# Attention in a hybrid block, written as one run of 64 items with the projections and the output stage beside them

## What is computed

```python
x = x + _L0_attn_a_ref(_layernorm(x), ...)      # a linear recurrence
x = x + _L0_ffn_ref(_layernorm(x), ...)         # top-k gated layer
x = x + _L0_attn_b_ref(_layernorm(x), ...)      # attention, below
x = x + _L0_ffn_ref(_layernorm(x), ...)

q = (x @ Wq.T).reshape(b, t, N_HEADS, HEAD_DIM)            # 8 heads of 64
kv_latent = x @ Wkv_down.T                                 # rank 64
k = (kv_latent @ Wk_up.T).reshape(b, t, N_HEADS, HEAD_DIM)
v = (kv_latent @ Wv_up.T).reshape(b, t, N_HEADS, HEAD_DIM)
scores = jnp.einsum('bqhd,bkhd->bhqk', q, k) * scale
attn = jax.nn.softmax(scores, axis=-1)
out = jnp.einsum('bhqk,bkhd->bqhd', attn, v)
return out.reshape(b, t, N_HEADS * HEAD_DIM) @ Wo.T
```

## Time and profile before

| | |
|---|---|
| median of 3 runs | 1613.02 us (1611.66 to 1614.74) |
| the profiled execution | 1612.51 us, its span 1610.8 us |
| TensorE busy | 1325.7 us, 82% of the span |
| VectorE busy | 1278.9 us, 79% |
| ScalarE busy | 1105.1 us, 69% |
| GpSimd busy | 1044.0 us, 65% |
| mean granted TensorE clock | 0.935 of full speed |

### The profile page before, as it was taken

One profiled execution on the slowest core, in us unless ns is written; L12 is line 12 of the kernel. 1 busy time (PEld: TensorE's weight loads), 2 busy tenths in 40 slices (PEclk: granted clock), 3 DMA queues, 4 the chain that ended last, 5 costly groups with the idle time before them and its releaser, 6 DMA issues.

```text
span 1610.8 us, 37935 instructions
## 1 busy us (share of the span) xinstructions
PE 1325.7 (82%) x10588; PEld 789.8 (49%) x10588; DVE 1278.9 (79%) x2953; ACT 1105.1 (69%) x2389; POOL 1044.0 (65%) x1234
## 2 busy tenths in 40 slices
PE   5888988767666679998799987999879998867675
PEld 2444444434344335656356663566635666444343
DVE  7988887379999669983689936899368994499997
ACT  3433431777777649995499954999549995888885
POOL 3456565258888738883388842888428885078887
PEclk9999999878988799999999999999999999989997
DMA  6000000000000000000000000000000000000000
GB/s 185 27 1 1 0 0 1 1 1 0 0 0 0 1 1 1 0 1 2 1 1 0 0 2 1 1 0 0 2 1 1 0 0 1 1 14 26 13 26 26
DMA packets 16972, 13.54 MB, mean 8 GB/s; under 512 B 5190, under 2 KB 16652, under 8 KB 16908
## 3 DMA queue, kind: packets, MB, share of 16 engines
q1 hardware_dynamic: 16908, 12.67, 2.6%
HBM read 8.47 MB, written 4.19 MB: 8 GB/s over the span
## 4 chain that ended last, share of the span: by engine, by line
issue 29%; PE 25%; DVE 24%; POOL 9%; ACT 7%; DVEq 3%; SPq 1%; DMA 1%; ACTq 1%; POOLq 0%
DVE arena L1319 5%; DVE arena L1219 4%; DVE arena L1214 4%; PE banks L1674 3%; DVE arena L1127 3%; PE banks L1595 3%; POOL arena L653 3%; PE banks L1614 2%; ACT arena L976 2%; POOL arena L648 2%; PE banks L1616 2%; PE banks L1527 2%; DVE arena L1339 2%; ACT arena L983 2%; PE banks L1580 2%
## 5 line engine op out<-in xcount | busy, mean ns | idle before, releaser
L653 POOL TENSOR_TENSOR arena<-arena 128x512 f16<-128x512 f32 x320 | 405.3, 1275 | 85.2 <-ACT arena L976 84.8
L983 ACT ACTIVATE arena<-banks 128x512 f32<-128x512 f32 x512 | 297.9, 595 | 65.9 <-PE banks L1616 56.2
L1319 DVE TENSOR_REDUCE arena<-banks 128x1 f32<-128x1024 f32 x256 | 307.1, 1216 | 19.6 <-PE banks L1595 10.3
L1339 DVE TENSOR_TENSOR arena<-arena 128x512 f16<-128x512 f32 x192 | 202.5, 1056 | 68.6 <-POOL arena L648 62.9
L976 ACT ACTIVATE arena<-arena 128x512 f16<-128x512 f32 x384 | 233.1, 624 | 0.0
L1629 PE MATMUL banks<-arena 128*128 128x65 f16 x2048 | 217.8, 197 | 13.8 <-POOL arena L653 13.7
L1630 PE MATMUL banks<-arena 128*128 128x64 f16 x2048 | 217.8, 193 | 0.0
L1629 PEld LDWEIGHTS banks<-arena 128*128 128x128 f16 x2048 | 192.2, 98 | 51.3 <-POOL arena L653 30.0
L1631 PE MATMUL banks<-arena 128*128 128x65 f16 x2048 | 216.8, 194 | 0.0
L1614 PE MATMUL banks<-arena 128*128 (+1 forms) x512 | 198.5, 388 | 10.8 <-ACT arena L983 10.8
L1219 DVE MATCH_REPLACE8 arena<-arena 128x256 f32<-128x256 f32 x512 | 205.3, 408 | 0.2
(11 more groups left out here) (196 smaller groups left out, 2931.4 us busy)
## 6 DMA issues: line engine op xcount, KB each, us to landing
x<-in_L_attn_a_x SPq DMA_DIRECT2D x8, 512.0 KB, 3.6
out<-x SPq DMA_DIRECT2D x8, 512.0 KB, 2.9
arena<-in_L_attn_a_W_in SPq DMA_DIRECT2D x1, 768.0 KB, 6.2
arena<-in_L_attn_a_W_mid SPq DMA_DIRECT2D x1, 512.0 KB, 6.9
arena<-in_L_attn_a_w_w SPq DMA_DIRECT2D x2, 256.0 KB, 7.1
arena<-in_L_attn_b_Wq SPq DMA_DIRECT2D x1, 512.0 KB
arena<-in_L_attn_b_Wo SPq DMA_DIRECT2D x1, 512.0 KB
fW<-in_L_ffn_weight SPq DMA_DIRECT2D x1, 256.0 KB
```

The lines of the kernel that those rows point to most:

```text
L653: nc.gpsimd.tensor_tensor(pr_lo[c][:, kt, :], pr[:, kt, :], pr_hi[c][:, kt, :], ALU.subtract).then_inc(a_lP, 1)
L983: nc.scalar.activation(pr[:, kt, :], ps[6 + kt % 2][:, :], ACT.Exp, scale=SM_SCALE).then_inc(a_P, 1)
L1319: nc.vector.tensor_reduce(mx[c][:, j:j + 1], psum[:, 2 * pair:2 * pair + 2, :].rearrange("p a b -> p (a b)"), X, ALU.max).then_inc(a_mx, 1)
L1339: nc.vector.tensor_tensor(pr_lo[c][:, kt, :], pr[:, kt, :], pr_hi[c][:, kt, :], ALU.subtract).then_inc(a_lD, 1)
```

## The change

The loop over batches and the loops inside it are written out: one run of 64 items W on every engine, with no loop instruction and with constants in the waits. The three parts of a batch are laid beside the items:
- The output stage of the batch behind: `FINAL_AT` names the item w of a batch (w = W mod 16) beside which row tile j of the batch behind is done: turned at kt = 1 on TensorE, copied at kt = 3 on ScalarE, multiplied at kt = 4, added at kt = 7 on VectorE.
- The queries of the next pair of heads, four items ahead (`QUERY_AT`, w = 0, 4, 8, 12), into a ring of four heads; turning, keys and latent rows of the batch ahead at w = 9, 10, 11, 13. The half c = 0 has its slot at kt = 1 (TensorE) and kt = 3 (ScalarE and VectorE), c = 1 at kt = 4, kt = 6 and kt = 7.
- The normalised rows of the batch ahead at w = 7 and 8 on ScalarE, kt = 6.
- Keys, latent rows and results (`kA`, `kB`, `latR`, `latL`, `o_sb`) have two buffers.
- The side work takes banks 2 and 3. `max_scores` writes into banks 0 and 1 alone, and waits for `largest_of` of the j right before it.

The prologue makes the projections of batch 0 with the first pair of heads only, and the output stage of batch 3 stands alone at the end as before. In batch 0 there is no output stage beside the items, in batch 3 no projection of a batch ahead. The statistics of the layer norm go straight into their place where the row number is a constant. The steps ahead of attention and behind it are as they were.

```diff
+GROUP = 4
+GROUPS = NH // 2
+Q_RING = 4
...
-        o_sb = xcT[:, :].rearrange("p (t d) -> p t d", t=TIME // P)
+        o_sb = [xcT[:, :].rearrange("p (t d) -> p t d", t=TIME // P), carve([TIME // P, NH * HD])]
...
         MX = TPC
-        Q_BANKS = (2, 3, 6, 7)
-
-
-        FIRST_LARGEST = {1: [(0, 0)], 2: [(0, 1)], 3: [(0, 2)], 4: [(0, 3)], 5: [(1, 0)], 6: [(1, 1)],
-                         7: [(1, 2), (1, 3)]}
-        FIRST_ROWS = 5
+        ALL = BATCH * ITEMS
+        FINALS = TIME // P
+
+
+        FINAL_AT = {1: 0, 2: 1, 3: 2, 5: 3, 6: 4, 7: 5, 14: 6, 15: 7}
+        QUERY_AT = {0: 1, 4: 2, 8: 3, 12: 4}
+        TURN_AT = {9: 0, 10: 1}
+        KEYS_AT, LATENT_AT = 11, 13
...
+            for W in range(ALL):
+                B, w = W // ITEMS, W % ITEMS
+                wait_from(pool, a_ops, W - 1)
+                high(W, 0)
+                low(W, 1)
+                low(W, 2)
+                high(W, 4)
+                if w in QUERY_AT and W + GROUP < ALL:
+                    pool.wait_ge(a_hP, high_done(W, 4))
+                    duplicate(B * GROUPS + QUERY_AT[w], 0)
+                low(W, 3)
+                low(W, 5)
+                if w == 6 and B:
+                    final_rstd(B - 1, 0)
+                if w == 1 and B > 1:
+                    final_rstd(B - 2, 1)
+                low(W, 7)
+                if w in QUERY_AT and W + GROUP < ALL:
+                    pool.wait_ge(a_lP, low_done(W, 7))
+                    duplicate(B * GROUPS + QUERY_AT[w], 1)
+            final_rstd(BATCH - 2, 1)
+            for half in range(2):
+                final_rstd(BATCH - 1, half)
...
+            for W in range(ALL):
+                B, w = W // ITEMS, W % ITEMS
+                onward = B + 1 < BATCH
...
+                    exps(W, kt)
                     if kt - 1 in HIGH_ACT:
-                        high(W, c, kt - 1)
...
+                        high(W, kt - 1)
+                    if kt == 3 and W + 1 < ALL:
+                        max_scaled(W + 1)
+                    if kt in (3, 6):
+                        c = kt // 6
+                        if w in FINAL_AT and B and c == 0:
+                            out_turned((B - 1) * FINALS + FINAL_AT[w], 2)
+                        if w in QUERY_AT and W + GROUP < ALL:
+                            query(B * GROUPS + QUERY_AT[w], c)
+                        if w in TURN_AT and onward:
+                            turned(B + 1, TURN_AT[w], c, 2 + c)
+                        if w == KEYS_AT and onward:
+                            keys(B + 1, c, 2 + c)
+                        if w == LATENT_AT and onward:
+                            latent(B + 1, c, 2 + c)
+                        if w in (7, 8) and onward and c:
+                            attn_rows(B + 1, w - 7)
+                    if kt == 5 and W + 1 < ALL:
+                        max_row(W + 1)
+                high(W, KT - 1)
...
+            for W in range(ALL):
+                B, w = W // ITEMS, W % ITEMS
+                onward = B + 1 < BATCH
...
+                    if kt % 2 == 0 and W + 2 < ALL:
+                        largest_of(W + 2, kt // 2)
...
+                        low(W, kt)
+                    if kt in (3, 7):
+                        c = kt // 7
+                        if w in FINAL_AT and B and c:
+                            final((B - 1) * FINALS + FINAL_AT[w], 3)
+                        if w in QUERY_AT and W + GROUP < ALL:
+                            query_low(B * GROUPS + QUERY_AT[w], c)
+                        if w == KEYS_AT and onward:
+                            keys_low(B + 1, c, 2 + c)
+                        if w == LATENT_AT and onward:
+                            latent_low(B + 1, c, 2 + c)
+                if W:
+                    normalise(W - 1)
+            normalise(ALL - 1)
+            for j in range(FINALS):
+                final((BATCH - 1) * FINALS + j, 6 + j % 2)
+
...
+            def out_final(J, bank):
+                B, j = J // FINALS, J % FINALS
+                pe.wait_ge(a_fe, J + 1)
+                if B == BATCH - 1:
+                    pe.wait_ge(a_fx, J - 1)
+                elif j in (0, 3):
+                    pe.wait_ge(a_ql, (((B + 1) * GROUPS + (1 if j == 0 else 2)) * 2 + 1) * 2 + 2)
...
+                for a in range(NH // 2):
+                    last = mm(ps[bank][:, 0:D], oT[J % 2][:, a, :], voB[:, a, :], start=a == 0,
+                              stop=a == NH // 2 - 1)
+                last.then_inc(a_fm, 1)
+
+            def max_scores(W, j):
+
+                B, hh, c, slot = place(W)
+                if j == 0:
+                    pe.wait_ge(a_kl, B * 2 + 2)
+                    pe.wait_ge(a_dup, query_done(W))
+                wait_from(pe, a_mx, W * MX + j)
                 for half in range(2):
-                    last = mm(ps[2 * pair + half][:, :], qA[:, bass.ds(hh, 1), c * CH + j * P:c * CH + j * P + P],
-                              kA[:, half * CH:half * CH + CH], start=True, stop=True)
+                    last = mm(ps[half][:, :], qA[:, slot, c * CH + j * P:c * CH + j * P + P],
+                              kA[B % 2][:, half * CH:half * CH + CH], start=True, stop=True)
                 last.then_inc(a_mps, 1)
...
+            for W in range(ALL):
+                B, w = W // ITEMS, W % ITEMS
+                onward = B + 1 < BATCH
                 for kt in range(KT):
-                    if kt in LARGEST_AT and largest:
-                        j = LARGEST_AT[kt]
-
-                        read = ((-1, 0, 1, 2) if before else (0, 0, 1, 2))[j]
-                        max_scores(W + 2, hh + 1, c, j, j % 2, read)
-                    scores(W, hh, c, kt)
-                    if kt in WEIGHTED_AT and before:
-                        weighted(W - 1, 1 - c, WEIGHTED_AT[kt])
-                    if kt == 5 and rows:
-                        max_row(W + 1, 1 - c)
...
+                    if kt % 2 == 0 and W + 2 < ALL:
+                        max_scores(W + 2, kt // 2)
+                    scores(W, kt)
+                    if kt in (1, 4):
+                        c = kt // 4
+                        if w in FINAL_AT and B:
+                            J = (B - 1) * FINALS + FINAL_AT[w]
+                            if c:
+                                out_final(J, 3)
+                            else:
+                                out_turn(J, 2)
+                        if w in QUERY_AT and W + GROUP < ALL:
+                            query(B * GROUPS + QUERY_AT[w], c)
+                        if w in TURN_AT and onward:
+                            turn(B + 1, TURN_AT[w], c, 2 + c)
+                        if w == KEYS_AT and onward:
+                            keys(B + 1, c, 2 + c)
+                        if w == LATENT_AT and onward:
+                            latent(B + 1, c, 2 + c)
+                    if kt in WEIGHTED_AT and W:
+                        weighted(W - 1, WEIGHTED_AT[kt])
+                    if kt == 5 and W + 1 < ALL:
+                        max_row(W + 1)
```

More of the change, by code:

```diff
@@ L973, in high @@
+            def high(W, kt):
+                c = W % 2
                 if kt == HIGH_ACT[0]:
-                    act.wait_ge(a_ops, W - 1 + CREDIT["a_ops"])
-                act.wait_ge(a_P, W * KT + (kt + 1 + CREDIT["a_P"]))
+                    wait_from(act, a_ops, W - 1)
+                act.wait_ge(a_P, W * KT + kt + 1)
                 nc.scalar.activation(pr_hi[c][:, kt, :], pr[:, kt, :], ACT.Copy).then_inc(a_hA, 1)
-            def step(W, hh, c, before, rows, largest):
+            for c in range(2):
+                attn_rows(0, c)
@@ new lines, in _ @@
+            for k in range(KB2):
+                turned(0, 0, k, k)
+            for k in range(KB2):
+                turned(0, 1, k, 2 + k)
+            for c in range(2):
+                keys(0, c, 4 + c)
+            for c in range(2):
+                query(0, c)
+            for c in range(2):
+                latent(0, c, 6 + c)
+            max_scaled(0)
+            max_row(0)
+            act.wait_ge(f_x, NT + CREDIT["f_x"])
+            for W in range(ALL):
+                B, w = W // ITEMS, W % ITEMS
+                onward = B + 1 < BATCH
@@ L1590, in max_scores, with turn @@
-            def max_scores(W, hh, c, j, pair=0, read=None):
-                pe.wait_ge(a_mx, W * MX + (j if read is None else read) + CREDIT["a_mx"])
+            def turn(B, c, k, bank):
+                n = LN_ATTN + B * 2 + c
+                pe.wait_ge(s_z, n + 1)
+                if B:
+                    if c == 0:
+                        pe.wait_ge(a_ql, query_done(B * ITEMS - 2 + k))
+                    else:
+                        pe.wait_ge(s_zT, n * 2 - 1 + k)
+                for j in range(TPC):
+                    last = nc.tensor.transpose(ps[bank][:, j * P:j * P + P], z_rows[c][:, j, k * P:k * P + P],
+                                               ident[:, :])
+                last.then_inc(s_tps, 1)
```

(47 more changed lines are left out.)

461 lines of the change are left out of this document (217 added, 244 removed).

## The result

The changed kernel takes 1724.8 us (median of 4 runs, 1722.8 to 1730.3) where the kernel before took 1612.3 in the runs beside it (median of 4, 1610.5 to 1614.7): 1.0702 times as long, 95% interval 1.0673 to 1.0731. The profiled execution took 1722.8 us, its span 1721.1.

What follows compares the result with a forecast made beforehand. Bound: nearly full engines, TensorE kept going by being one `max_scores` ahead of VectorE. Forecast: 1612.5 + 108 (loop with side work) - 9 (start) + 19 (contention) + 40 (clock) = 1770 us; range 1640 to 1840 holds 0.8.

Steps and rivals of the forecast that it cites:

- The bound and the direction: In attention's items, one pair of banks makes TensorE wait for VectorE's first maximum, closing a three-engine loop; slower, chance 0.86.
- the signs that the prediction named: TensorE waiting about 1.9 us at L1736, plain items near 10.4, busy under 80% in items, clock under 0.97.
- The plain period: An item without side work takes 10.4 us instead of 8.65: 6.49 of TensorE's stretch plus 3.95 behind the scores.
- The other maxima don't add: Within an item, maxima after the first cost nothing: 1.8 us each, beside about 2 us of TensorE's work.
- The way over ScalarE: Loop's stretch from kt = 7's scores: 0.26 to the exponential, 0.49 to kt = 6's high part, 0.62 for it.
- The side work: Items take 13.7 us beside outputs (1.1 waiting for oT), 15.1 queries, 11.35 turning, 13.85 keys, 12.85 latent rows.
- The sum: Four batches of items: 197, 228.3 for each full one, 212, less 7; 858 against 750, a loss of 108 us.
- The clock: TensorE at half clock for 3.4 us behind long gaps, 27 times: 40 us taken, bounds 0 and 90.
- The contention: GpSimd's and VectorE's low parts collide at kt = 6: 0 to 0.7 us an item, 0.3 taken, 19 us in all.
- The start and the end: Shorter prologue, with two of eight query products, gains 9 us before the first exponential; nothing forecast for the end.
- Side work hides: Rival: in items only TensorE's 1.75 us adds; 742 us, total 1596 to 1655; chance 0.12 for 1618 to 1690.
- Overlap pays: Rival: maxima don't stall TensorE, whose own work bounds items at 8.65 us; about 1535 us; chance 0.08.

Runs made afterwards that it cites:

- the run without side work: Changed kernel without any side work, one pair of banks: 1520.3 us; its counterpart with two pairs took 1395.3 us.
- first reordered versions: Changed kernel with normalise and next item's first maximum ahead of kt = 6's low part, 1619.5 us; plus copy to oT at kt = 2 and later VectorE side work, 1609.4.
- the one with the early copy alone: Changed kernel with ScalarE's copy of the turned result to oT at kt = 2 instead of kt = 3: 1710.7 us.
- the later ones: Changed kernel, VectorE reordered, plus copy to oT at kt = 2 and later side work, 1609.4 us; plus fourth maximum moved, 1600.7; plus normalised rows singly, 1591.1.
- the reordered versions: Changed kernel with VectorE's first maximum ahead of kt = 6's low part, alone or with further edits: 1619.5, 1609.4, 1600.7 and 1591.1 us.
- the version with the fourth maximum moved: Changed kernel, VectorE reordered, copy to oT at kt = 2, later side work, and fourth maximum ahead of kt = 4's low part: 1600.7 us.

## Why the prediction was right, and where it was not

*The bound and the direction.* Right. One `max_scores` ahead of VectorE was what kept TensorE going: with one pair alone the kernel before loses 102 us, and the run without side work 117 us in its items. Of the signs that the prediction named, one failed and one held barely: TensorE is busy 82 to 83% in the items and not under 80%, and its clock is 0.95 to 0.97 there.

*The plain period.* 10.4 forecast, 10.34 measured; the stretch behind the scores is 3.82 us instead of 3.95. "The other maxima don't add" was wrong. The chain leads over GpSimd and through the fourth maximum into the last low part, and the first `max_scores` waits 0.73 us for that maximum. The way over ScalarE, which the prediction took, is about as long: on ScalarE's timeline the high parts of kt = 6 and 7 start at 638.30 and take 1.14 us together, so the first ends near 638.9, and the low part starts at 638.96 (0.3 us are between the two in the item before). So the number comes out, with some luck: the loop that was forecast is there, but in plain items it is not the one that ended last. In the first reordered versions the fourth maximum is what is left, and costs 0.9 us an item. Whether another order on GpSimd would shorten that way wasn't run.

*The side work.* An item beside an output takes 13.31 us (13.7 forecast), with TensorE waiting 0.8 us at L1724 in 9 of the 24, 1.1 and 1.2 in two others and next to nothing in the rest (1.1 forecast for each). Turning takes 11.33 at w = 10 (11.35), keys 12.84 (13.85). Items with queries take 13.4 to 14.7 and not 15.1 (15.6 to 16.0 at w = 8 and, behind the statistics, at w = 0 of batches 2 and 3), but the stall of their second half falls into the next item, which takes 13.6 to 13.8 where a plain one takes 10.34: the two together 27.0 to 27.7 in batch 0, 25.5 forecast.

*The sum.* The batches took 201.8, 223.5, 228.4 and 204.2 us where 197, 228.3, 228.3 and 205 (212 less the last two items' 7) were forecast: 857.9 against 858. (To the end of the last high part, as the prediction counts the 750 before, it is 858.9, 109 us over.) That the sums agree so well is luck in part: batch 0 is 5 us over its forecast, batch 1 is 5 under. And the measured batches hold the contention and the clock, for which the prediction added 59 us on top. This is the step that was mis-sized, and 1770 is 47 us more than the profiled execution took: without these 59 the sum is 1711, and with 1 more in the batches, 3 less gained at the start and 7 at the end it is 1723.

*The clock.* 40 us forecast (0 to 90). The mechanism is there: 0.55 behind the gap of 3.76 us, 72 us of the items at the lower level, in 14 stretches, against 27 us in 5 before. The forecast had 27 stretches of 3.4 us on top of those; 9 came, 45 us more. At half clock TensorE can lose half of that, 22 us at most (an estimate). Windows over the whole attention step, before and after:

```profile
549.10:1377.00 827.90, 749.17 (x8699) 462.72 (x8698) 606.75 (x766) 621.68 (x1212) 536.42 (x558) 0.97 0.00 1
```

```profile
549.10:1480.00 930.90, 762.47 (x8695) 483.39 (x8695) 593.35 (x755) 614.40 (x1208) 509.98 (x556) 0.94 0.01 1
```

The same matmuls take 762.5 us instead of 749.2, 13 us more. That isn't the clock's cost by itself, since TensorE's busy time also grows with gaps alone: between the two versions without side work, both at 1.00, from 8.44 to 8.82 us an item. So no run separates what the clock cost; it is about half of the forecast at most.

*The contention.* 19 us forecast, for low parts that meet at kt = 6. That doesn't happen: none of the 64 there takes over 0.75 us. The meeting that does happen is at kt = 4 (1.63 us in the first timeline above), and it isn't new: those of the kernel before take over 0.8 us in all 64 items, those of the changed kernel in 58. It lies on the chain through the fourth maximum and is in the 10.34 us already.

*The start and the end.* The first exponential is at 591.4 us instead of 597.0: 5.6 gained, 9 forecast. Only 2.3 of them are the shorter prologue (29.1 us from the first query product, now 26.9); the others lie ahead of attention. Behind the last high part 270.8 us pass where 263.7 did, which the prediction had at nothing: 1.6 of these 7 lie ahead of the last step. In the last step, which the change doesn't touch, the other 5.4 us are waits of ScalarE for VectorE. In the version with VectorE's order alone changed, and in the one with the early copy alone, 0.1 and 0.5 of them are left, in the later ones 2 to 4, with the same instructions there. Their cause wasn't found. So 1612.5 + 109 - 5.6 + 7 = 1722.9.

*The rivals.* "Side work hides" had 742 us for the items instead of 858; it doesn't hide. "Overlap pays" decides, as the prediction says, by how far VectorE's first maximum is behind the scores of kt = 7, and with the reordered versions that bound was moved and the sign changed: in plain items of the version with the fourth maximum moved it starts 1.5 us behind them, where the prediction asked for less than 2.0. (By its own terms that rival saves some 65 us in the items, not 69, and comes to about 1539.) The Trainium skill, Perfetto Trace Analysis, section Identifying Performance Opportunities, says that a gap which repeats on the engine that should be saturated can mean too few buffers. The traces agree: without side work TensorE has 93 us of such gaps with one pair, between 590 and 1230 us, and with two pairs a single gap, of 0.2 us, between 600 and 1100 us.

## What to carry to other kernels

Before side work gets its banks from a double buffer, follow the loop that this closes: from the write into the single buffer over every instruction that stands ahead of its reader on the reader's engine, back to the writer. If that is longer than the period, either keep the buffer or put the reader first in its engine's order; here the order alone was worth 105 us, 94 of them in the items. Keeping the buffer together with the side work wasn't run. And follow every engine that feeds the reader: in plain items the chain went over GpSimd, which the prediction had left out. A cost that isn't in a loop's chain (a collision, a slower clock) should be added only as far as it makes that chain longer, not as a sum of its own.

## What was not expected of the hardware

The lower clock follows gaps very unevenly. Gaps of 0.73 to 0.75 us, twice an item, leave the clock at 1.00 through 640 us (the version with one pair and no side work), while one gap of 3.76 us brings 3.5 us at 0.55. Moving one copy of ScalarE made a wait in the items beside outputs shorter and the time at the lower clock longer, 92 us instead of 72, which no run here explains.
